# Cross weights turned in ten full blocks per tile, and the work ahead of the loop in another order

## The reference

```
m = silu(cond) @ w_ada + b_ada          # nine sections: shift, scale, gate, three times
x += g_msa * self_attn(ln(x) * (1+sc) + sh)     # 16 heads of 16, windows of 128 tokens, rolled by 64
x += g_mca * cross(ln(x) * (1+sc) + sh, ctx)    # 16 heads, 77 keys, only the 16 largest scores kept
x += g_mlp * swiglu(ln(x) * (1+sc) + sh)        # 256 -> 2 x 1024 -> 256
# second block, on tokens of 8 x 512
nx = ln(x);  evidence = softmax(nx Wq (protos Wk)^T / 16) (protos Wv);  comb = [nx, evidence, anchor]
routed = sum_e softmax(comb @ router_W + router_b)_e * (silu(comb @ e_w1[e] + e_b1) @ e_w2[e] + e_b2)
x += sigmoid(silu(comb @ gate_w1 + b) @ gate_w2 + b) * (routed @ out_w + out_b)
```

## Time and profile before

| | before |
|---|---|
| median of 3 runs | 1445.8 us (1445.67, 1445.8, 1449.09) |
| span of the profiled execution | 1447.1 us |
| PE busy | 1413.0 us, 98% |
| DVE busy | 1061.7 us, 73% |
| ACT busy | 837.8 us, 58% |
| POOL busy | 437.8 us, 30% |

### The profile page before, as it was taken

The page is one execution under the profiler, slowest core; times in us unless marked ns, Lnnn a source line. Parts: engine busy times, 40 slices in busy tenths (PEclk is TensorE's granted clock), DMA queues, the critical chain, the costliest instruction groups (busy, mean ns, idle before and its releaser), DMA issues.

```text
span 1447.1 us, 30246 instructions
## 1 busy us (share of the span) xinstructions
PE 1413.0 (98%) x9777; PEld 1195.1 (83%) x9777; DVE 1061.7 (73%) x4754; ACT 837.8 (58%) x2555; POOL 437.8 (30%) x599
## 2 busy tenths in 40 slices
PE   7999999999999999999999999999999999999997
PEld 5778788888888888888888788888888878887886
DVE  3585869688796878879696777959688786968642
ACT  3464475757566384755757466574757547574433
POOL 1314132333325232332335232233334313232302
PEclk9999999999999999999999999999999999999999
DMA  7520000010000000010010000000010000000000
GB/s 244 196 73 2 1 1 25 1 34 9 19 31 15 1 2 25 2 34 2 21 36 2 15 2 16 11 15 20 8 43 8 16 2 1 9 2 8 1 2 14
DMA packets 27342, 34.99 MB, mean 24 GB/s; under 512 B 3325, under 2 KB 22449, under 8 KB 26930
## 3 DMA queue, kind: packets, MB, share of 16 engines
q1 hardware_dynamic: 27185, 33.07, 7.1%
HBM read 28.83 MB, written 4.22 MB: 23 GB/s over the span
## 4 chain that ended last, share of the span: by engine, by line
PE 83%; DVE 12%; issue 2%; ACT 1%; SPq 0%; POOL 0%; DMA 0%; DVEq 0%; ACTq 0%; POOLq 0%
PE bank L965 13%; PE bank L920 12%; PE bank L989 10%; PE bank L972 7%; PE bank L791 6%; PE bank L929 6%; PE bank L777 4%; PE bank L852 4%; PE bank L840 4%; PE bank L904 4%; DVE knocked L2224 3%; PE bank L830 2%; PE bank L748 2%; PE bank L762 2%; PE bank L812 1%
## 5 line engine op out<-in xcount | busy, mean ns | idle before, releaser
L920 PE MATMUL bank<-hB,Wm 128*128 128x256 f32 x1024 | 242.3, 383 | 2.2 <-ACT hB L1366 2.2
L920 PEld LDWEIGHTS bank<-hB,Wm 128*128 128x128 f32 x1024 | 190.6, 190 | 33.4 <-issue 7.0
L965 PE MATMUL bank<-nxT,W1nx 128*128 128x256 f32 x896 | 212.1, 382 | 0.0
L1405 ACT ACTIVATE prob<-bank,rmax 128x128 f32<-128x128 f32 x512 | 180.3, 432 | 28.3 <-DVE rmax L2151 28.3
L1762 POOL TENSOR_TENSOR scores<-scores,M 128x308 f32<-128x308 f32 x128 | 94.5, 738 | 320.1 <-DVE knocked L2224 317.7
L1412 ACT ACTIVATE probT<-bank 128x512 f32<-128x512 f32 (+1 forms) x256 | 140.3, 617 | 83.8 <-PE bank L904 76.8
L989 PE MATMUL bank<-W2p,gT 128*128 128x256 f32 x768 | 183.2, 381 | 3.0 <-DVE acc L2303 1.9
L965 PEld LDWEIGHTS bank<-nxT,W1nx 128*128 128x128 f32 x896 | 166.1, 191 | 23.1 <-issue 2.8
L989 PEld LDWEIGHTS bank<-W2p,gT 128*128 128x128 f32 x768 | 141.2, 190 | 23.8 <-issue 2.8
L1450 ACT ACTIVATE tbs<-bank,b1half 128x256 f32<-128x256 f32 x128 | 60.7, 474 | 143.1 <-PE bank L920 102.2
L1466 ACT ACTIVATE tbs<-bank,betaH 128x256 f32<-128x256 f32 x224 | 95.6, 489 | 82.7 <-PE bank L972 82.7
(11 more groups left out here) (238 smaller groups left out, 2772.4 us busy)
## 6 DMA issues: line engine op xcount, KB each, us to landing
Wm_g<-in_L_xcond_w_m_dram SPq DMA_DIRECT2D x4, 1024.0 KB, 5.4
W1ev<-in_L_xcond_e_w_dram SPq DMA_DIRECT2D x6, 512.0 KB, 7.2
x<-in_x_dram SPq DMA_DIRECT2D x16, 128.0 KB, 2.6
x<-in_x_dram SPq DMA_DIRECT2D x32, 64.0 KB, 2.3
Wm<-in_L_xcond_w_m_dram SPq DMA_DIRECT2D x1, 2048.0 KB, 9.3
out_dram<-acc SPq DMA_DIRECT2D x16, 128.0 KB, 1.7
out_dram<-acc SPq DMA_DIRECT2D x32, 64.0 KB, 2.0
batch_rows<-row_store SPq DMA_DIRECT2D x4, 384.0 KB, 3.9
```

The source lines that it names most:

```text
L920: m = pe.matmul(bank_of(name)[:, half * UT:(half + 1) * UT], Wm1[:, k, c:c + P], hB[:, k, :], start=(k == 0), stop=(k == CB - 1))
L965: pe.matmul(bank_of(name)[:, n * UT:(n + 1) * UT], W1nx[:, k, c0 + n * P:c0 + (n + 1) * P], nxT[:, k, :], start=(n == 0 and k == 0), stop= ...
L1405: m = act.activation(prob[:, s, i, :], psum[s][:, i * P:(i + 1) * P], ACT.Exp, bias=rmax[:, t, s * HPS + i:s * HPS + i + 1], accum_out=rsu ...
```

## The change

Two edits are made together.

The cross scores lie in pairs of heads, each pair padded from 154 to 160 columns with zeros, so the 16 heads of a tile take 1280 columns, ten blocks of 128. TensorE turns these ten blocks whole instead of sixteen heads; slot 1's turn is dropped, and the banks of slots 0, 2 and 3 take 4, 4 and 2 blocks. ACT makes three copies instead of four. A block mixes rows of several heads, so the values are laid out to match: for each pair two blocks of 128 rows, in which only the rows of the head in question are filled. The vector engine copies the values to `value_rows`, and twelve DMAs per batch of runs of 16 numbers place them in `vc` (`place_values`), for which TensorE waits (`values_placed`). `scores` and the larger `vc` are set to zero once at the start on GpSimd. Searches, shift, exponential and pick go by the padded layout.

In `prologue()` the order is another one on TensorE, ACT and DVE: the scores of tile 0 of unit 0 come ahead of the context's values and of "mR", their maxima right behind the queries; the turns of tile 0 and the folds alternate in another way; "b01" is folded between the two tiles' cross scores of unit 0 instead of ahead of the scores of tile 1; its bias, the halving and the reading of "wk" stand among the searches; the maxima of unit 1 come earlier among them; `fold_second` is split in halves; some fillers are dropped.

```diff
 LC = 77
+HEAD_PAIR = 160
+CROSS = 8 * HEAD_PAIR
...
     ("s13", 1), ("pv", 1), ("p10", 1), ("p11", 1), ("p12", 1), ("p13", 1), ("r1", 1), ("y00", 0),
-    ("y01", 0), ("y02", 0), ("y03", 0), ("so", 1), ("r2", 0), ("xv", 0), ("y10", 0), ("y11", 0),
+    ("y02", 0), ("y03", 0), ("so", 1), ("r2", 0), ("xv", 0), ("y10", 0),
...
+PLACED = 16 * 12
...
+CROSS_BLOCKS = {0: (0, 1, 2, 3), 2: (5, 6, 7, 8), 3: (4, 9)}
+CROSS_AT = {blk: at for at, blk in enumerate(CROSS_BLOCKS[0] + CROSS_BLOCKS[2] + CROSS_BLOCKS[3])}
...
 kc = sb("kc", [P, PAR, CB, LC])
-vc = sb("vc", [LC, H // PAR, 2 * PAR * D])
+vc = sb("vc", [P, H // PAR, 2, PAR * D])
+value_rows = sb("value_rows", [LC, C])
...
 prob = sb("prob", [P, SLOTS, HPS, P])
-scores = sb("scores", [P, TILES * H * LC])
-S = scores[:, :].rearrange("p (t h c) -> p t h c", t=TILES, h=H)
+scores = sb("scores", [P, TILES * CROSS])
...
+
+def cross_heads(t, h0, h1):
+
+    return pairs[:, t, h0 // PAR:h1 // PAR, 0:PAR * LC]
 def own_half(v):
...
         sp.dma_start(batch_rows[:, n0:n1, :].rearrange("p n c -> p (n c)"), src).then_inc(loaded, 16)
+
+    def place_values(b):
+
+        sp.wait_ge(values_read, b + 1)
+        alone(sp)
+        for low in range(SLOTS):
+            s, f, first = low // CB, low % CB, 32 * low
+            for e in range(PAR):
+                at, n = first + e * LC, 0
+                while n < LC:
+                    blk, row = (at + n) // P, (at + n) % P
+                    m = min(LC - n, P - row)
+                    head = 8 * f + 2 * s + e
+                    src = value_rows[n:n + m, :].rearrange("c (h d) -> c h d", d=D)[:, head:head + 5:4, :]
+                    sp.dma_start(vc[row:row + m, low:low + 5:4, blk, e * D:(e + 1) * D], src).then_inc(values_placed, 16)
+                    n += m
     def load_wm2():
         sp.dma_start(Wm2_g[:, :, :], blocks(w_m2)).then_inc(wm2_loaded, 16)
...
                     m.then_inc(full[s], 1)
     def a_turn_picked(t, s, u):
-        if s % 2 == 0:
-            pe.wait_ge(picked, u * (TILES * 2) + (2 * t + s // 2 + 1))
+        pe.wait_ge(picked, u * (TILES * 2) + (2 * t + (s > 0) + 1))
         wait_free(pe, f"y{t}{s}", u)
-        for i in range(HPS):
-            m = pe.transpose(psum[s][0:LC, i * P:(i + 1) * P], Dx[:, t, s * HPS + i, :], ident[:, :])
+        for i, blk in enumerate(CROSS_BLOCKS[s]):
+            c = t * CROSS + blk * P
+            m = pe.transpose(psum[s][:, i * P:(i + 1) * P], scores[:, c:c + P], ident[:, :])
         m.then_inc(full[s], 1)
     def a_cross_values(t, u):
-        weigh_values("xv", "y", vc[:, :, :], LC, t, u)
+
+        if t == 0:
+            wait_free(pe, "xv", u)
+        for s in CROSS_BLOCKS:
+            wait_drained(pe, f"y{t}{s}", u)
+        for f in range(CB):
+            for half in range(2):
+                for s in range(SLOTS):
+                    pair = CB * s + f
+                    blk = CROSS_AT[pair * HEAD_PAIR // P + half]
+                    m = pe.matmul(bank_of("xv")[32 * s:32 * s + 32, f * UT + t * P:f * UT + (t + 1) * P],
+                                  vc[:, pair, half, :], probT[:, blk // HPS, blk % HPS, :],
+                                  start=(half == 0), stop=(half == 1))
+        if t == TILES - 1:
+            m.then_inc(full[JOB["xv"][0]], 1)
     def b_hidden(j, u):
...
         a_k(0)
         a_q(0)
         a_v(0, 0)
+        a_v(1, 0)
+        a_scores(0, range(SLOTS), 0)
         context_values(0, fold_bank("cV"))
-        a_v(1, 0)
         modulations("mR", (4, 3, 7, 6))
-        a_scores(0, range(SLOTS), 0)
+        a_turn_probs(0, 0, 0)
         value_biases()
+        a_turn_probs(0, 1, 0)
         gate_sections("g25", (0, 1))
-        a_turn_probs(0, 0, 0)
-        a_turn_probs(0, 1, 0)
+        a_turn_probs(0, 2, 0)
         gate_sections("g8", (2,))
-        a_turn_probs(0, 2, 0)
+        a_turn_probs(0, 3, 0)
         fold_turn_second(0, 1)
-        a_turn_probs(0, 3, 0)
         fold_turn_second(0, 0)
-        fold_expert_biases("b01", (0, 1))
         a_scores(1, range(SLOTS), 0)
         a_values(0, 0)
         fold_anchor(0)
         a_turn_probs(1, 0, 0)
-        idle_in_values(3)
+        fold_second(0, 0, (0,))
         a_turn_probs(1, 1, 0)
-        fold_second(0, 0)
+        fold_second(0, 0, (1,))
         a_turn_probs(1, 2, 0)
+        fold_second(0, 1, (0,))
         a_turn_probs(1, 3, 0)
-        fold_second(0, 1)
+        fold_second(0, 1, (1,))
         a_values(1, 0)
         a_turn_inverses("r1", "pv", 0)
...
         pe.wait_ge(q2_loaded, 16)
         a_query(0)
         fold_expert_biases("b2", (2,))
-        fold_turn("wk", wk_sb)
         pe.wait_ge(readA, 2)
         a_cross_scores(0, range(SLOTS), 0)
+        a_turn_input(1)
+        fold_expert_biases("b01", (0, 1))
+        a_cross_scores(1, range(SLOTS), 0)
         wait_free(pe, "pv", 1)
-        idle_in_values(2)
-        a_turn_input(1)
-        idle_in_values(5)
-        a_cross_scores(1, range(SLOTS), 0)
         idle_in_values(2)
         a_q(1)
         a_k(1)
         a_v(0, 1)
+        a_v(1, 1)
+        fold_turn("wk", wk_sb)
         fold_second(1, 1)
-        a_v(1, 1)
+        a_scores(0, range(SLOTS), 1)
         fold_second(1, 0)
-        a_scores(0, range(SLOTS), 1)
         fold_turn("wq", wq_sb)
         fold_turn_second(2, 0)
         fold_turn_second(2, 1)
-        fold_qk()
         a_turn_probs(0, 0, 1)
-        fold_router_anchor()
-        idle_in_values(2)
+        idle_in_values(3)
         a_turn_probs(0, 1, 1)
         idle_in_values(3)
         a_turn_probs(0, 2, 1)
         idle_in_values(3)
         a_turn_probs(0, 3, 1)
-        idle_in_values(6)
+        fold_qk()
+        fold_router_anchor()
         a_scores(1, range(SLOTS), 1)
         a_values(0, 1)
         fold_second(2, 1)
+        a_turn_probs(1, 0, 1)
         fold_second(2, 0)
-        a_turn_probs(1, 0, 1)
         a_turn_probs(1, 1, 1)
         a_turn_probs(1, 2, 1)
         fold_router_rows()
...
         a_turn_inverses("r1", "pv", 1)
         a_values(1, 1)
         a_turn_picked(0, 0, 0)
-        a_turn_picked(0, 1, 0)
         a_turn_picked(0, 2, 0)
         a_turn_picked(0, 3, 0)
         a_project("pv", oT, "so", Wso_g, 1)
         a_turn_inverses("r2", "xv", 0)
-        pe.wait_ge(values_read, 1)
+        pe.wait_ge(values_placed, PLACED)
         a_cross_values(0, 0)
         a_turn_picked(1, 0, 0)
-        a_turn_picked(1, 1, 0)
         a_turn_picked(1, 2, 0)
         a_turn_picked(1, 3, 0)
         idle_products(4)
...
-        wait_full(act, name, u)
-        act.activation(probT[0:np_, s], psum[s][0:np_, :].rearrange("p (i q) -> p i q", i=HPS), ACT.Copy)\
+    def a_copy_turned(t, s, u):
+        wait_full(act, f"p{t}{s}", u)
+        act.activation(probT[:, s], psum[s][:, :].rearrange("p (i q) -> p i q", i=HPS), ACT.Copy)\
+           .then_inc(drained[s], 1)
+
+    def a_copy_picked(t, s, u):
+        wait_full(act, f"y{t}{s}", u)
+        n, at = len(CROSS_BLOCKS[s]), CROSS_AT[CROSS_BLOCKS[s][0]]
+        act.activation(probT[:, at // HPS, 0:n], psum[s][:, 0:n * P].rearrange("p (i q) -> p i q", i=n), ACT.Copy)\
            .then_inc(drained[s], 1)
...
-        act.activation(Dx[:, t, g], Dx[:, t, g], ACT.Exp, scale=float(D) ** -0.5).then_inc(cross_exp, 1)
+        g = cross_heads(t, half * (H // 2), (half + 1) * (H // 2))
+        act.activation(g, g, ACT.Exp, scale=float(D) ** -0.5).then_inc(cross_exp, 1)
...
         g = slice(s * HPS, (s + 1) * HPS)
-        pool.tensor_tensor(Dx[:, t, g, :], S[:, t, g, :], M12[:, t, g, 0:1].to_broadcast([P, HPS, LC]), ALU.subtract)\
+        v = cross_heads(t, s * HPS, (s + 1) * HPS).rearrange("p n (e c) -> p n e c", e=PAR)
+        top = M12[:, t, g, 0:1].rearrange("p (n e) a -> p n e a", e=PAR).to_broadcast([P, HPS // PAR, PAR, LC])
+        pool.tensor_tensor(v, v, top, ALU.subtract)\
...
     pool.memset(va[:, :, :, :], 0.0).then_inc(consts, 1)
-    pool.memset(vc[:, :, :], 0.0).then_inc(consts, 1)
+    pool.memset(vc[:, :, :, :], 0.0).then_inc(consts, 1)
+    pool.memset(scores[:, :], 0.0).then_inc(consts, 1)
     pool.memset(bias3[:, :, :], 0.0).then_inc(consts, 1)
-    pool.wait_ge(consts, 8)
...
         alone(dve)
-        dve.tensor_copy(own_half(vc[:, :, :]), bk[0:LC, 0:C].rearrange("p (n e d) -> p n e d", e=PAR, d=D)).then_inc(values_read, 1)
...
-            src, top = (S[:, t, h, :], M12[:, t, h, 0:8]) if first else (K[:, h, :], M12[:, t, h, 8:TOPK])
+            src, top = (cross_head(t, h), M12[:, t, h, 0:8]) if first else (K[:, h, :], M12[:, t, h, 8:TOPK])
             dve.match_replace(K[:, h, :], top, src, KNOCKED).then_inc(topk, 1)
     def a_pick(t, half, u):
         dve.wait_ge(cross_exp, u * (TILES * 2) + (2 * t + half + 1))
         dve.wait_ge(topk, u * TOPK_PER_UNIT + max(topk_base("b", t, s) for s in (2 * half, 2 * half + 1)) + 2 * HPS)
-        g = slice(half * (H // 2), (half + 1) * (H // 2))
```

(59 more changed lines are left out.)

145 lines of the change are left out of this document (68 added, 77 removed), and 2 rows, old and new, of the table BANK_JOBS.

## The result

| | before | after |
|---|---|---|
| median of 5 runs | 1448.93 us (1445.67 to 1451.94) | 1455.75 us (1455.13 to 1459.97) |
| ratio of the runs, 95% interval | | 1.0051 (1.0034 to 1.0068) |
| span of the profiled execution | 1447.1 us | 1453.9 us |

The change is slower by half a per cent, about 7 us, where 1444.0 and a small gain were predicted. The two profiled executions differ by 6.8 us. Five marks cut them into sections: the first search on the vector engine, the router row's addition, TensorE's first MLP block of the loop, the r2 turn of the last unit, the end.

The account below looks back on a forecast made before the run. Each iteration was taken as a vector-bound half up to r2, then a TensorE-bound half. The profiled 1447.1 us, front -1.3, last unit -0.5, loop 0, gave 1445.3; taken as 1.3 above the median, 1444.0, range 1435 to 1451.

Parts of the forecast that it names:

- Rival D: In front of the loop: late first gates, r1 turn +0.9 and a half-clock pause cost +3 us, giving 1448; 12%.
- The loop: Removed transposes save 1.31 us per unit, but TensorE waits that much longer at or before r2: gain 0.
- the 0.5 of the last unit: Last unit: its twelve removed transposes could pay up to 1.3 us; the forecast took -0.5.
- the signs of being right: TensorE about 20 us less busy, idle a microsecond or more before r2 in 14 units, vector half unchanged at 40.3.
- rival A: Removed transposes pay: all of it gives 1424 us (7%), a part with the front about 1438 (16%).
- Rival B: In the loop, new pauses before r2 lower TensorE's clock, costing 1.7 us in each of 14 iterations: 1468; 5%.
- Rival C: Segments cost the vector engine 0.25 us in each of 64 picks, 16 us in all: 1460; 4%.
- Placing and zeroing: Value transfers take about 7 us per batch, hidden in the loop by 19; zeroing scores takes 2.4, hidden. Cost 0.
- The searches start at 67.04 ... I take no change: In front, a 0.5 us later r1 turn is offset by moved vector work; start stays between 66.4 and 67.2.
- Maxima and edits ahead push the router row to about 102.9: In front, maxima and edits among the searches delay the router row's addition from 99.73; TensorE's router turn waits for it.
- So moves from 105.60 to about 106.5: In front, the r1 turn, issued behind the waiting router turn, comes 0.9 us later.
- the -0.9 behind it: In front, behind that r1 turn, the pause with fillers ahead of the second cross values shrinks by about 0.9 us.

Follow-up runs that it names:

- before_q: The kernel before, with the self attention queries' bias and scale moved in the loop from the vector to the scalar engine: 1444.25 us, ratio 0.9978.
- part1_q: part1 with the self attention queries' bias and scale moved in the loop from the vector to the scalar engine: 1436.38 us, ratio 0.9917.
- part1_q_pad: part1_q with six more useless transposes per tile in every unit, ahead of the third block bank's copy: 1450.34 us, ratio 1.0024.
- part2: The kernel before with only the new prologue order; sixteen transposes, four copies and the old value writing stay: 1458.8 us, ratio 1.0070.
- front_both: The changed kernel with the old order at the start and unit 1's values copied ahead of the cross exponentials: 1453.04 us, ratio 1.0018.
- front_va: The changed kernel with the scalar engine's copy of unit 1's values ahead of the first cross exponential: 1452.34 us, ratio 1.0037.
- part1: The changed kernel with the old prologue order; ten blocks, placed values and zeroed scores stay: 1447.15 us, ratio 0.9994 to the kernel before.
- tail_pad: part1 with six more useless transposes per tile in the last unit alone: 1448.83 us, ratio 1.0001.
- both_q: front_both with the queries' bias of units 2 to 15 moved to the scalar engine: 1438.72 us, ratio 0.9936.

## Why the prediction was wrong

The median missed the forecast by 11.75 us: 6.5 at the loop's first block (131.96, forecast 125.5), 0.4 in the loop, 1.7 in the tail and 3.1 in the base of the sum. Rival D (late gates, a pause, the half clock) named what went wrong in front, but at +3; the front lost 5.2.

**The loop: right.** 192 transposes went, 20.9 us of work by the forecast, and none of it came out in the time, nor did the 0.5 of the last unit. The records are a poor measure of it: the loop has 180 matmuls fewer (8515 to 8335) and 9.6 us less busy time (1222.26 to 1212.70), half of 180 x 0.109. A transpose's record lasts 282 ns where the next one starts after 0.11 us, so a short wait can hide in it; that this is the whole difference isn't shown. So two of the signs of being right came too small, 10.4 us of busy time over the whole span instead of about 20 and 0.84 us at r2 instead of a microsecond or more. The vector-bound half kept its 40.30 us, the wait is where it was put, and rival A was refuted in the loop as it stands and shown right for a loop with less on the vector engine (before_q, part1_q, part1_q_pad). Rival B did not come: with pauses of 0.84 us the stretches on both sides of r2 stand at a granted clock of 1.00, and the one fall that the last unit has ahead of its r2 turn is there before, too. The rule of the Trainium skill cited there ("TensorE: Matmul & The Clock Gate", "A second HAM failure mode: psum-queue depth-cycling") is not borne out at this size of pause either. Rival C did not come: 793 ns.

**Placing and zeroing: right in cost, wrong in size.** Twelve issues took 10.19 us where 4.6 were estimated from one large load; the 19 us of cover were enough. By the Trainium skill, "DMA: Bandwidth & Descriptors", section "Specifications", transfers under 512 bytes don't reach line rate; the trace shows long issues and no landing, so no run here shows whether that holds for these. The zeroing took 2.23 us (estimate 2.4), and was hidden.

**"The searches start at 67.04 ... I take no change": failed, +2.95, in part by chance.** The step moved the first r1 turn by 0.5 us for the gate rows' delay and went no further. The turn came 2.4 us later. Of these 1.6 were there when the first projections ended, ahead of every changed place in TensorE's list: their sixteen matmuls took 5.74 us against 4.32, and in other kernels anything between (sixteen of the same shape take 3.69 at 73.71). The granted clock reads 1.00 there in both kernels, so it doesn't explain this. The other 0.8 is the delay that was forecast, somewhat larger. What the step missed is that TensorE has nothing to do there but wait: 1.41 us, after which the clock fell and the projection took 3.20 us instead of 1.97, more in part2 (3.76). All four profiles with the changed order wait there and have the long projection, none of the six with the order of before; their searches start at 69.85 to 72.55 and at 65.68 to 69.89. So the direction is shown, and the size is not. Nor does the old order keep the clock up by itself: in front_both the wait is 0.61 us and the projection took 3.17.

**"Maxima and edits ahead push the router row to about 102.9": too small.** Of the section's 4.47 us, 2.0 are the edits that were counted (busy time 32.32 to 34.29). The other 2.5 is idle time: the vector engine waits 2.59 us in its list for scores that TensorE had not made. They were late by TensorE's 2.08 us wait for the copied values, which the scalar engine had behind the reading of a fold, and TensorE's list had moved that fold back. The step moved the maxima forward on the vector engine and didn't ask whether their input comes forward too. front_va takes 2.13 us of the wait away with one line.

**"So moves from 105.60 to about 106.5", and the -0.9 behind it: failed.** With the row at 107.15 TensorE waits 4.15 us, and the r1 turn follows the row by 5.1 us. The forecast's own figures (102.9 to 106.5) leave 3.6 for this and give no reason: from the router turn to the r1 turn it took 4.81 us, as before (4.83), at a granted clock of 0.50 both times. Of the -2.2 behind the r1 turn the transposes gave 1.2 of their 1.3 us (part1, r1 turn to first block 19.96 against 21.18), and the fillers 0.3 of 0.9 (part2, 20.91).

**The tail: failed, +1.67.** The mechanism is a clock of 0.64 in 1385 to 1388 us, behind the same two pauses (0.97 and 2.19 us) that before has at full clock. The forecast had no term for it. All ten kernels with the blocks have a tail of 93.55 to 93.78 us, all three without 92.08 to 92.09. It isn't TensorE's load there (tail_pad, part1_q_pad), and TensorE's work from r2 to those pauses has the same times. The clock differs already ahead of r2: an earlier stretch at 0.50 begins 15.2 us ahead of the last r2 turn before and 17.4 us after. The stretches of before, then of after, with the tail's last:

```profile
1339.80:1343.20 3.40, 3.40 (x14) 3.13 (x13) 3.40 (x29) 0.36 (x1) 0.84 (x2) 0.50 0.00 0
```

```profile
1342.80:1349.60 6.80, 6.57 (x24) 5.61 (x24) 6.80 (x53) 2.77 (x6) 1.42 (x3) 0.50 0.01 2
...
1385.00:1388.00 3.00, 3.00 (x11) 2.45 (x10) 0.00 (x0) 0.75 (x2) 0.00 (x0) 0.64 0.00 0
```

Whether that has to do with it wasn't tried, so what decides the tail stays open.

**The base.** The sum took the profile's 1447.1 us to stand 1.3 above the median. In every run the measured time is 1.8 us above the span of the same execution (1455.75 and 1453.9). So 1447.1 belongs to a run of about 1449, the middle of what before does.

## What to carry to other kernels

A wait that an engine already has is the first thing to read: work removed ahead of it turns into more of it. To find out if such work is lost or only waiting, take a little off the other engine, with and without the change. And when lists written by hand are reordered, each moved instruction has to be asked two questions, whether its input moves along on the other engines' lists, and what stands behind it if it does not.

## What the runs showed of the hardware

The granted clock falls behind some of TensorE's pauses and not behind others like them: behind the tail's 2.19 us in ten kernels, and not in three. In front of the loop falls cost as much as most of the edits tried here: the same lists (front_both and both_q, up to the first search) took 71.92 and 64.15 us. Runs of one kernel differ by up to 9 us (part1_q, 1432.16 to 1441.11), while the loop takes 1227.88 to 1228.43 us in all nine profiles without the queries moved. So a gain of 2 us in front shows in a profile's sections before it shows in a median. And an issue of many runs of 64 bytes on the sync engine's queue took 0.66 to 1.74 us, against 0.44 for the weight load behind it.
